# Activation quantisation of an FFN: scaling, int32 conversion and PSUM copies given to ScalarE, in quarters of 1024 columns

## The reference

```python
def _act_quant(x):                       # per token (row)
    scale = 127.0 / jnp.clip(jnp.max(jnp.abs(x), axis=-1, keepdims=True), 1e-05)
    xq = jnp.clip(jnp.round(x * scale), -128.0, 127.0) / scale
def _bitlinear(x, w):
    return jnp.einsum('bsi,oi->bso', _act_quant(x), _weight_quant(w))
gate = jax.nn.silu(_bitlinear(x, w_gate))       # 1024 -> 4096
up = _bitlinear(x, w_up)                        # 1024 -> 4096
ffn = _bitlinear(gate * up, w_down)             # 4096 -> 1024
xn = _layernorm(x); s = attn(xn, ...); g = _silu(ffn(xn)); x = x + s * g
```

## Time and profile before

| what | us |
|---|---|
| two timed runs | 15487.4 and 15590.4 |
| their median | 15538.9 |
| profiled execution | 15457.1 |
| span of its slowest core (of 15397.7 to 15455.5) | 15455.5 |
| FFN, 11628.0 to the end | 3827.5 |

### The profile page before, as it was taken

How to read it: one execution, slowest core, us unless ns; L and a number is a source line. 1 busy time by engine, 2 the same in 40 slices (tenths; PEclk the granted TensorE clock), 3 DMA queues, 4 the chain that set the end, 5 groups by cost and what they waited for, 6 DMA issues and landing times.

```text
span 15455.5 us, 103841 instructions; the slowest of 8 cores (15397.7 to 15455.5 us)
## 1 busy us (share of the span) xinstructions
PE 7869.9 (51%) x30860; PEld 3317.6 (21%) x30860; DVE 6238.9 (40%) x7134; ACT 1470.8 (10%) x1680; POOL 614.4 (4%) x1028
## 2 busy tenths in 40 slices
PE   1104666665666655256666666666554543444534
PEld 0101222222222221122222222222211211111211
DVE  5634444444444430344444444444204223443233
ACT  0011111111111110111111111111000000000000
POOL 4610000000000000000000000000000000000000
PEclk9998888888888876577888888888666776777766
DMA  5540000000000011100000000000111221112211
GB/s 170 164 108 23 4 7 4 7 4 4 7 4 7 4 34 36 44 13 7 4 4 7 4 7 4 5 6 4 40 36 57 83 87 60 61 65 76 87 66 60
DMA packets 237094, 569.99 MB, mean 37 GB/s; under 512 B 41731, under 2 KB 115588, under 8 KB 219014
## 3 DMA queue, kind: packets, MB, share of 16 engines
q1 hardware_dynamic: 187398, 454.24, 9.3%
q0 software_dynamic: 49152, 109.12, 2.4%
HBM read 454.16 MB, written 109.05 MB: 36 GB/s over the span
## 4 chain that ended last, share of the span: by engine, by line
PE 46%; DVE 32%; DMA 8%; issue 8%; ACT 4%; DVEq 2%; ACTq 1%; SPq 1%; POOL 0%; POOLq 0%
PE P L693 5%; PE P L694 5%; PE P L695 5%; DVE t_El L174 4%; PE P L1142 3%; PE P L1147 3%; PE P L850 3%; DVE t_rc L174 3%; ACT t_Ef L174 3%; DVE t_qs L174 3%; DVE t_Eh L174 2%; PE P L852 2%; PE P L851 2%; DVE t_qr L174 2%; PE P L1270 2%
## 5 line engine op out<-in xcount | busy, mean ns | idle before, releaser
L693 PE MATMUL P<-t_xn2h,t_winh 128*64 128x512 bf16 x3072 | 1337.1, 435 | 1570.1 <-DVEq L175 1550.7
L174 DVE CAST t_Eh<-t_Ef 128x1024 bf16<-128x1024 f32 x1024 | 710.9, 694 | 2549.5 <-ACTq L175 2246.9
L694 PE MATMUL P<-t_xn2l,t_winh 128*64 128x512 bf16 x3072 | 1324.4, 431 | 0.0
L850 PE MATMUL P<-t_Eh,t_vth 128*65 128x512 bf16 x2048 | 833.1, 407 | 944.2 <-DVEq L175 942.7
L695 PE MATMUL P<-t_xn2h,t_winl 128*64 128x512 bf16 x3072 | 1306.9, 425 | 0.0
L174 DVE TENSOR_TENSOR t_El<-t_Ef,t_Eh 128x1024 bf16<-128x1024 f32 x1024 | 1254.6, 1225 | 80.2 <-issue 3.0
L174 ACT ACTIVATE t_Ef<-P 128x1024 f32<-128x1024 f32 x512 | 524.4, 1024 | 4298.0 <-PE P L826 4241.7
L693 PEld LDWEIGHTS P<-t_xn2h,t_winh 128*64 128x64 bf16 x3072 | 380.4, 124 | 2163.7 <-issue 1926.1
L852 PE MATMUL P<-t_El,t_vth 128*65 128x512 bf16 x2048 | 840.9, 411 | 0.0
L851 PE MATMUL P<-t_Eh,t_vtl 128*65 128x512 bf16 x2048 | 840.2, 410 | 0.0
L174 ACT ACT_TABLE_LOAD x80 | 102.6, 1283 | 7383.2 <-PE P L826 2805.3
(11 more groups left out here) (132 smaller groups left out, 10084.4 us busy)
## 6 DMA issues: line engine op xcount, KB each, us to landing
t_wgb<-wgT_s SPq DMA_DIRECT2D x64, 1024.0 KB, 4.9
t_wub<-wuT_s SPq DMA_DIRECT2D x64, 1024.0 KB, 7.1
t_wdb<-wdT_s SPq DMA_DIRECT2D x512, 128.0 KB, 2.1
t_wt<-wg SPq DMA_DIRECT2D x64, 512.0 KB, 4.2
t_wt<-wu SPq DMA_DIRECT2D x64, 512.0 KB, 4.2
t_wt<-wd SPq DMA_DIRECT2D x64, 512.0 KB, 4.6
t_Xt<-x SPq DMA_DIRECT2D x32, 512.0 KB, 3.5
xn_s<-t_xnt POOLq DMA_DIRECT2D x32, 512.0 KB, 2.9
```

The source lines that it names most:

```text
L174: _a(*args, **kw)
L693: tensor.matmul(ps, lh, rh, start=(c == 0), stop=False)
L694: tensor.matmul(ps, lh, rl, start=False, stop=False)
L850: tensor.matmul(P3[0:65, :], vh, eh, start=st, stop=False)
```

## The change

It touches the two quantisations of the FFN and nothing else.

- `f_q` and `f_hq` are split in three. A DVE section makes the scales (`f_qs`, `f_hqs`). An ACT section (`f_qa`, `f_hqa`) makes `t_y` and `t_i32` with two ACTIVATE operations of the function Copy, both from the input tile, with the scale read from `t_fq` and a constant bias of 512. A second DVE section (`f_qr`, `f_hqr`) does the subtraction, the comparison and the last combination.
- The `h` tile is worked in quarters of 1024 columns instead of halves of 2048: `f_hqa`, `f_hqr`, `f_trh`, `f_evh` are emitted for quarter 0, then for quarter 1, and so on. Two halves of `t_y` and `t_i32` alternate.
- The copies from `P2b` (`f_evx`, `f_evh`) are done by ACT, with Copy, instead of by DVE. The transposes wait for the ACT counter as well, and the first `dmm` matmul waits for the last ACT copy of the `h` tiles.
- `f_qs` waits for the load alone; the wait for PE that `f_q` had at its head stands in `f_qr`.

The diff, cut to its core:

```diff
-                def f_q(vector, tt=tt, par=par, ldt=LD.tok(), mmn=MM.n, cc=cc):
+                def f_qs(vector, tt=tt, par=par, ldt=LD.tok()):
                     LD.wait(vector, ldt)
-                    if cc > 0 or tt > 0:
-                        vector.wait_ge(MM.h, mmn)
...
-                    vector.tensor_scalar(t_y[:, 0:1024], xc, t_fq[:, cb + 1:cb + 2],
-                                         512.0, OP.mult, OP.add)
-                    vector.tensor_copy(t_i32[:, 0:1024], t_y[:, 0:1024])
...
+                qs = 1024 * (tt % 2)
+                def f_qa(scalar, tt=tt, par=par, qs=qs, vvn=VV.n, vvf=VV.n):
+                    scalar.wait_ge(VV.h, vvn)
+                    xc = t_xnc[par][:]
+                    cb = 8 * tt
+                    scalar.activation(t_y[:, qs:qs + 1024], xc, AF.Copy,
+                                      bias=512.0, scale=t_fq[:, cb + 1:cb + 2])
+                    AA.inc(scalar.activation(t_i32[:, qs:qs + 1024], xc, AF.Copy,
+                                             bias=512.0,
+                                             scale=t_fq[:, cb + 1:cb + 2]))
+                sec("scalar", f_qa)
+
+                def f_qr(vector, tt=tt, qs=qs, aan=AA.n, mmn=MM.n, cc=cc):
+                    vector.wait_ge(AA.h, aan)
+                    if cc > 0 or tt > 0:
+                        vector.wait_ge(MM.h, mmn)
...
-                def f_evx(vector, tt=tt, mmn=MM.n):
-                    vector.wait_ge(MM.h, mmn)
+                def f_evx(scalar, tt=tt, mmn=MM.n):
+                    scalar.wait_ge(MM.h, mmn)
...
-                    VV.inc(vector.tensor_copy(dst, src))
-                sec("vector", f_evx)
+                    AA.inc(scalar.activation(dst, src, AF.Copy,
+                                             bias=0.0, scale=1.0))
+                sec("scalar", f_evx)
...
+                r_t = {}
+                for qq in range(4):
+                    hs = 1024 * (qq % 2)
+                    def f_hqa(scalar, tt=tt, qq=qq, hs=hs, cb=8 * tt,
+                              vvn=r_t.get(qq - 2, 0) or VV.n):
+                        scalar.wait_ge(VV.h, vvn)
+                        hsl = t_h[tt][:, 1024 * qq:1024 * qq + 1024]
+                        scalar.activation(t_y[:, hs:hs + 1024], hsl, AF.Copy,
+                                          bias=512.0,
+                                          scale=t_fq[:, cb + 6:cb + 7])
+                        AA.inc(scalar.activation(t_i32[:, hs:hs + 1024], hsl,
+                                                 AF.Copy, bias=512.0,
+                                                 scale=t_fq[:, cb + 6:cb + 7]))
+                    sec("scalar", f_hqa)
+
+                    def f_hqr(vector, tt=tt, qq=qq, hs=hs, aan=AA.n):
+                        vector.wait_ge(AA.h, aan)
+                        ys = t_y[:, hs:hs + 1024]
+                        i32s = t_i32[:, hs:hs + 1024]
+                        vector.tensor_sub(ys, ys, i32s)
+                        vector.tensor_single_scalar(t_c01[:, 0:1024], ys,
+                                                    0.5, OP.is_gt)
+                        VV.inc(vector.scalar_tensor_tensor(
+                            t_hq[:, 1024 * qq:1024 * qq + 1024], i32s,
+                            -512.0, t_c01[:, 0:1024], OP.add, OP.add))
+                    sec("vector", f_hqr)
+                    r_t[qq] = VV.n
...
-                    def f_evh(vector, tt=tt, grp=grp, mmn=MM.n):
-                        vector.wait_ge(MM.h, mmn)
-                        dst = t_hqT[tt][:, 1024 * grp:1024 * grp + 1024]
-                        VV.inc(vector.tensor_copy(dst, P2b[:]))
-                    sec("vector", f_evh)
+                    def f_evh(scalar, tt=tt, qq=qq, mmn=MM.n):
+                        scalar.wait_ge(MM.h, mmn)
+                        dst = t_hqT[tt][:, 1024 * qq:1024 * qq + 1024]
+                        AA.inc(scalar.activation(dst, P2b[:], AF.Copy,
+                                                 bias=0.0, scale=1.0))
+                    sec("scalar", f_evh)
...
+            aa_hqT = AA.n
...
                     def f_dmm(tensor, o=o, i=i, ip=ip, ldt=LD.tok(), vvn=vv_hqT,
-                              aa_d0=aa_d0, aan=AA.n):
+                              aa_d0=aa_d0, aah=aa_hqT):
```

More of the change, by code:

```diff
@@ L1071, in f_q @@
                                       t_scal[:, 1:2])
-                    vector.tensor_mul(t_fq[:, cb + 4:cb + 5], t_fq[:, cb + 2:cb + 3],
-                                      t_scal[:, 3:4])
-                    vector.tensor_scalar(t_y[:, 0:1024], xc, t_fq[:, cb + 1:cb + 2],
-                                         512.0, OP.mult, OP.add)
-                    vector.tensor_copy(t_i32[:, 0:1024], t_y[:, 0:1024])
-                    vector.tensor_sub(t_y[:, 0:1024], t_y[:, 0:1024], t_i32[:, 0:1024])
@@ L1078, in f_q @@
-                    vector.tensor_single_scalar(t_c01[:, 0:1024], t_y[:, 0:1024],
+                    VV.inc(vector.tensor_mul(t_fq[:, cb + 4:cb + 5],
+                                             t_fq[:, cb + 2:cb + 3],
+                                             t_scal[:, 3:4]))
+                sec("vector", f_qs)
+                qs = 1024 * (tt % 2)
[8 more added lines that the diff above has]
+                                             scale=t_fq[:, cb + 1:cb + 2]))
@@ L1079, in f_q @@
+                sec("scalar", f_qa)
[3 more added lines that the diff above has]
+                        vector.wait_ge(MM.h, mmn)
+                    ys = t_y[:, qs:qs + 1024]
+                    i32s = t_i32[:, qs:qs + 1024]
+                    vector.tensor_sub(ys, ys, i32s)
+                    vector.tensor_single_scalar(t_c01[:, 0:1024], ys,
                                                 0.5, OP.is_gt)
-                    VV.inc(vector.scalar_tensor_tensor(t_xq[:], t_i32[:, 0:1024],
-                                                       -512.0,
-                                                       t_c01[:, 0:1024], OP.add, OP.add))
@@ L1083, in emit_xnquant, with f_trx @@
-                sec("vector", f_q)
+                    VV.inc(vector.scalar_tensor_tensor(t_xq[:], i32s, -512.0,
+                                                       t_c01[:, 0:1024],
+                                                       OP.add, OP.add))
+                sec("vector", f_qr)
                 if cc == 0 and tt == 0:
                     tap_dump("xq0", t_xq[:], [(VV, VV.n)])
-                def f_trx(tensor, tt=tt, vvn=VV.n, vve=VV.n):
+                def f_trx(tensor, tt=tt, vvn=VV.n, aae=AA.n):
@@ L1088, in f_trx @@
                     tensor.wait_ge(VV.h, vvn)
+                    if aae:
+                        tensor.wait_ge(AA.h, aae)
                     for c in range(8):
@@ L1182, in build_program, with f_hqs @@
             for tt in range(4):
-                def f_hq(vector, tt=tt, mmn=MM.n, cc=cc, aan=AA.n):
+                def f_hqs(vector, tt=tt, mmn=MM.n, cc=cc, aan=AA.n):
                     cb = 8 * tt
@@ L1199, in f_hq @@
                                                 OP.mult)
[L1200 to L1222, removed]
+                    VV.inc(vector.tensor_mul(t_fq[:, cb + 7:cb + 8],
+                                             t_fq[:, cb + 5:cb + 6],
+                                             t_scal[:, 5:6]))
+                sec("vector", f_hqs)
@@ new lines, in build_program, with f_trh @@
+                r_t = {}
[16 more added lines that the diff above has]
+                        i32s = t_i32[:, hs:hs + 1024]
+                        vector.tensor_sub(ys, ys, i32s)
+                        vector.tensor_single_scalar(t_c01[:, 0:1024], ys,
+                                                    0.5, OP.is_gt)
[4 more added lines that the diff above has]
+                    r_t[qq] = VV.n
+                    def f_trh(tensor, tt=tt, qq=qq, vvn=VV.n, aae=AA.n):
@@ L1223, in f_trh @@
                         tensor.wait_ge(VV.h, vvn)
+                        tensor.wait_ge(AA.h, aae)
                         for c in range(8):
-                            ci = 8 * grp + c
+                            ci = 8 * qq + c
                             ins = tensor.transpose(P2b[:, 128 * c:128 * c + 128],
@@ L1230, in build_program @@
                     sec("tensor", f_trh)
-                    def f_evh(vector, tt=tt, grp=grp, mmn=MM.n):
-                        vector.wait_ge(MM.h, mmn)
-                        dst = t_hqT[tt][:, 1024 * grp:1024 * grp + 1024]
-                        VV.inc(vector.tensor_copy(dst, P2b[:]))
-                    sec("vector", f_evh)
+                    def f_evh(scalar, tt=tt, qq=qq, mmn=MM.n):
[4 more added lines that the diff above has]
+                    sec("scalar", f_evh)
+                if cc == 0 and tt == 0:
+                    tap_dump("hq0", t_hq[:], [(VV, VV.n)])
             vv_hqT = VV.n
+            aa_hqT = AA.n
             if cc + 1 < N_CC:
@@ L1265, in f_dmm @@
```

(2 more changed lines are left out.)

## The result

| | before | changed kernel |
|---|---|---|
| median of the timed executions, us | 15516.7 (10) | 16043.0 (11) |
| ratio | 1 | 1.034, 95% interval 1.029 to 1.039 |
| span of the profiled execution, us | 15455.5 | 16066.7 |
| first load of `t_xnc` (the FFN starts), us | 11628.5 | 11783.4 |
| FFN, from there to the end, us | 3827.0 | 4283.3 |

The change makes the kernel 3.4% slower; 15965 was forecast, in a range of 15850 to 16150, with the sum of the parts at 474 us. On the slowest cores the FFN is 456 us longer. The other 155 us of the two spans lie ahead of the FFN, in code that the change doesn't touch: in a second profile of the same kernel the cores of one die had a lower granted clock there (0.785 to 0.787) than those of the other (0.808 or 0.809) and started the FFN at 11758 to 11778 us, the others at 11627 to 11647, and all of them took 4269 to 4290 us for the FFN.

The account below looks back on a forecast made before the run. The FFN's two quantisations were taken as serial chains, about 1450 us or 9% of the span. Serial quarters and table loads add 474 us to 15457.1, giving 15931, plus 30 for the base: 15965 forecast, range 15850 to 16150.

Parts of the forecast that it names:

- The order decides: FFN quantisation: ACT's in-order queue puts the next quarter's ACTIVATEs behind this quarter's copy, so quarters run serially.
- The quarter: One h quarter: ACTIVATEs 1.11 us each, DVE 3.29, transposes 1.18, copy 1.02, plus handoffs; tile 37.73 us without loads.
- the 1.2 us less that was foreseen there: Block 0: the three later h maxima need not wait for PE, -3.5 us together.
- The table loads: Each ACT section loads a table: 400 instead of 80, 1.283 us each, 7 on an h tile's path, 46.71 us per tile.
- Copy sections without a load: Rival: new ACT sections holding only Copy get no table load; time 15631 us, 0.9% up; chance 0.13.
- The dearer load: Rival: before a load ACT drains the previous operation on the path, 284 us more, 16249 us; chance 0.03.
- The phase: Per block with loads: h phase 189.0 us against 132.4, input tiles 51.1 against 48.5, 59.2 longer together.
- The sum: Whole FFN, eight blocks: 474 us longer with table loads, 144 without.
- the last block: Eighth block, no input tiles behind its h tiles: 189.4 us with loads against 129.2, 60 longer.
- The base: Profiled execution of the kernel before, 15457.1 us; 30 added because the middle of three executions lies that much higher.
- The third rival: ACT gets ahead and h quarters overlap: about 19.5 us per tile, 403 us faster, 15085 us; chance 0.02.
- Costed at nothing: Outside the quantisations: PE's clock, SP's order, POOL's stores and the rest taken as unchanged, no term.

Follow-up runs that it names:

- e2: Changed kernel with ACT making the next quarter's ACTIVATEs before the copy, and a tile's maximum not waiting for the previous transposes; ratio to the kernel before 0.998.
- e8: Kernel before, nothing on ACT, h tiles in quarters on DVE, each copy behind the next quarter's arithmetic; ratio to the kernel before 0.999.
- e1: Changed kernel with all ACT operations of a block's two quantisations in one ACT section, same order and waits; ratio to the kernel before 1.010.
- e4: Changed kernel with the h tiles' PSUM copies back on DVE and a tile's maximum not waiting for the previous transposes; ratio to the kernel before 1.005.
- e5: Changed kernel with each ACT section of two ACTIVATEs split into two sections, 160 more sections; ratio to the kernel before 1.048.
- e3: Changed kernel with the edits of e1 and e2 together, merged ACT sections and reordered ACT queue; ratio to the kernel before 0.985.
- e6: e3 plus next tile's maximum before DVE's last quarter, ACT two quarters ahead across tiles, input loads waiting only for their buffer's last reader; ratio to kernel before 0.969.

## Why the prediction was right, point by point

- **The order decides.** Right, and shown by e2: same sections and loads, ACT's queue reordered, 529 us of FFN time gone, of which the moved wait can hold some 25 (1.2 us at three borders in each of blocks 1 to 7).
- **The quarter.** The ACTIVATE with a scale took 1.147 us, not 1.11, the same for float32 and int32 output. The copy took 1.024 (1.02). DVE to PE took 0.28 us (12522.38 to 12522.66) where the earlier trace rows had 0.17. The transposes' section now begins with two waits, for its quarter and for the copy before; in e8, where it has one, the handoff is 0.17 again (12409.95 to 12410.12), in e1 with two it is 0.27 (12387.75 to 12388.02). Whose counters they are makes no difference: in e4 both are for DVE's counter (but for a block's first quarter) and the handoff is 0.28 as well. PE to ACT took 0.08 to 0.1 where 0.15 had been read, the section change 0.20 to 0.21 where 0.26 had been taken. Per tile that is 0.30 too little for the ACTIVATEs and 0.44 for DVE to PE, 0.21 too much for PE to ACT and 0.18 for the section changes. That they nearly cancel is luck: tile period 47.08 for 46.71, and 45.9 for two of the three in block 0, the 1.2 us less that was foreseen there.
- **The table loads.** 400, as forecast, at 1283 ns, behind the section's first wait. The chance of 0.13 for Copy sections without a load is refuted. The rule in the Trainium skill, ScalarE: Activation LUTs, section Table sets: the hidden batching unit, that functions of one set need no second load, holds inside a section (e1: a single load for all the Copy operations of a block) and not across sections. What the Trainium skill, ScalarE activation tables: per-element evaluation and per-set limits, section Table sets in the compiler and the runtime, says, that loads are placed per block, agrees with all the kernels here, if a section is such a block. The dearer load (its chance was 0.03) is refuted as well: in e5 a load starts 0.15 us behind an ACTIVATE of 1.15.
- **The phase.** 190.3 against 189.0 for the `h` phase. The input tiles took 41.1 us from first to fourth maximum against 3 x 13.23 = 39.7, since the single periods of blocks 1 to 7 run from 13.3 to 15.3 us where each was taken at 13.23: the maxima waited up to 5.4 us for their loads where the earlier trace rows had 3.46.
- **The sum.** 7 x (190.3 - 132.1) = 407, the input 8 x 1.6 = 13, the last block 61 (60 forecast), together 481, against 474. The stretch of `dmm` and `gmm` adds a little that the forecast had at nothing: by the median of the cores it averages 281.7 us before and 284.8 and 282.9 in the two profiles of the changed kernel, 10 to 25 us over eight blocks. That gives 491 to 506, and the FFN's 499 lies in it. The 456 of the slowest cores come out lower because the kernel before had two of these stretches at the lower granted clock.
- **The base.** 30 us were added for the kernel before standing higher than its profiled execution; over ten executions its median stood at 15516.7, 60 above it. That is some 30 of the 78 us between 15965 and 16043. The other 50 are the gap between the medians' difference, 526, and the sum of 474: 25 of them are the FFN's (499), the rest lies well inside the interval of the ratio, by which the true difference is 456 to 599 us.
- **The third rival.** It had priced overlapping quarters without loads at 19.5 us per tile. With that order and no loads e3 took 24.7: it has DVE wait 2.69 us for the first ACT section of a tile, and 0.32, 1.57 and 0.53 us ahead of the other quarters, which the price left out. Over the tiles' borders, in e6, it is 21.8.
- **Costed at nothing:** `gmm` and `dmm` kept their length but for the 1 to 3 us per block above, so SP's and POOL's order cost no more than that there. DVE gave up 308 us of busy time (6238.9 to 5931.0), which brought nothing, since the time was on one chain whichever engine it ran on.

What stays open: where those 1 to 3 us per block come from, and why some input loads land later in the changed kernel.

## What to carry to other kernels

Moving work to an idle engine pays only if that engine's queue lets it run ahead: write down the order in which the receiving engine meets its own operations, and look for one that waits, over other engines, for the very step whose successor is queued behind it. Here the move lost 3.4% in one order, lost nothing in another with the same operations and loads (e2), and won 1.5% once the sections were merged as well (e3), 3.1% with DVE kept busy over the borders (e6). Where each short section brings a fixed cost (here a table load of 1.28 us), count sections, not operations, and keep an engine's work of a phase in one section.

## What was not expected of the hardware

- A section that holds only Copy reloads the table even if the one before it was a Copy section: 560 loads for 480 new and 80 old sections in e5.
- An ACTIVATE of 128x1024 with a scale read from memory costs 1147 ns for float32 and int32 outputs alike.
- DVE (1.23 us) and ACT (1.15 us) operations on the same tiles kept their durations when they ran side by side in e2, e3 and e6.
- A second wait at the head of PE's section came with 0.11 us more of handoff from DVE, even where both waits are for the same engine (0.28 in e4, 0.17 in e8).
